# The attention-weighted sum of a windowed attention: one product of 64 keys per query block instead of two of 32

## What is computed

```python
# reference, cut: one layer of the macaron stage (DEPTH = 6 of them, run twice)
def attn_layer(x, Wqkv, qs, ksc, Wo):
    q, k, v = split(shift_tokens(x) @ Wqkv)         # 16 heads x 64
    q, k = rotary(l2norm(q) * qs), rotary(l2norm(k) * ksc)
    # windows of 32 tokens: a query block sees its own block and the one before it
    bk2, bv2 = look(blocks(k)), look(blocks(v))     # 64 keys for each block of 32 queries
    attn = softmax(where(mask, -max, einsum('bhwie,bhwje->bhwij', blocks(q), bk2) * 8.0))
    out = einsum('bhwij,bhwje->bhwie', attn, bv2)   # the product that is changed
    return merge(out) @ Wo
x = attn_layer(shift_tokens(x), ...) + x
x = ffn_layer(shift_tokens(x), ...) + x             # (a * gelu(gate)) @ W2
```

## Time and profile before

| | us |
|---|---|
| median of 3 executions | 4348.66 |
| lowest, highest | 4320.82, 4349.43 |
| the profiled execution, its own time | 4339.44 |
| span of the profiled execution | 4337.7 |
| first scores of the first and of the second macaron stage, from the span's start | 64.0, 1857.1 |
| granted TensorE clock, mean over the span | 0.959 |

### The profile page before, as it was taken

How to read it: one execution, slowest core, us unless ns; L and a number is a source line. 1 busy time by engine, 2 the same in 40 slices (tenths; PEclk the granted TensorE clock), 3 DMA queues, 4 the chain that set the end, 5 groups by cost and what they waited for, 6 DMA issues and landing times.

```text
span 4337.7 us, 161987 instructions
## 1 busy us (share of the span) xinstructions
PE 4006.5 (92%) x70897; PEld 2563.2 (59%) x70897; DVE 3070.5 (71%) x5228; ACT 2752.8 (63%) x4932; POOL 2741.4 (63%) x3746
## 2 busy tenths in 40 slices
PE   5999999999999999589999999999999976999985
PEld 3666666666666666356666666666666654333333
DVE  6777777777777776577777777777777744577744
ACT  3767677777767676167777767676777742366652
POOL 5877787777777776388777777777777750000000
PEclk8999999999999999799999999999999987599997
DMA  3000000000000000000000000000000000000000
GB/s 85 5 5 25 10 25 5 10 25 9 5 25 10 25 5 10 21 4 10 25 5 9 25 10 5 25 10 25 5 10 5 5 3 0 0 1 1 1 1 10
DMA packets 75304, 53.56 MB, mean 12 GB/s; under 512 B 48472, under 2 KB 71400, under 8 KB 72944
## 3 DMA queue, kind: packets, MB, share of 16 engines
q1 hardware_dynamic: 74608, 43.28, 3.6%
HBM read 35.93 MB, written 1.05 MB: 9 GB/s over the span
## 4 chain that ended last, share of the span: by engine, by line
PE 75%; DVE 13%; ACT 4%; issue 4%; POOL 3%; DVEq 0%; SPq 0%; POOLq 0%; DMA 0%; ACTq 0%
PE psum L339 12%; PE psum L404 8%; PE psum L350 8%; PE psum L361 8%; PE psum L423 7%; PE psum L386 5%; DVE turn L635 4%; PE psum L415 4%; PE psum L1155 3%; PE psum L503 3%; PE psum L493 3%; PE psum L486 3%; PE psum L1124 2%; DVE den L672 2%; PE psum L1143 2%
## 5 line engine op out<-in xcount | busy, mean ns | idle before, releaser
L635 DVE TENSOR_TENSOR turn<-psum,ropes 128x512 f32<-128x512 f32 x1536 | 946.5, 674 | 82.0 <-POOL qkr L736 53.3
L743 POOL TENSOR_TENSOR turn<-turn 128x1024 f32<-128x1024 f32 x384 | 903.7, 2376 | 8.3 <-DVE turn L635 8.2
L522 ACT ACTIVATE sq<-psum 128x512 f32<-128x512 f32 x768 | 455.5, 593 | 543.9 <-PE psum L339 543.9
L339 PE MATMUL psum<-wqkv,xT 128*128 128x512 f32 x1536 | 769.3, 624 | 8.6 <-DVE turn L635 6.6
L736 POOL TENSOR_TENSOR qkr<-turn,rn 128x1024 f32<-128x1024 f32 x384 | 727.2, 1914 | 1.0
L770 POOL TENSOR_TENSOR scratch<-scratch,rden 128x1024 f32<-128x1024 f32 x192 | 365.3, 1903 | 467.3 <-DVE rden L675 467.3
L404 PEld LDWEIGHTS psum<-scratch,V 32*64 32x64 f32 x29952 | 546.6, 132 | 182.4 <-issue 181.3
L404 PE MATMUL psum<-scratch,V 32*64 32x64 f32 (+1 forms) x29952 | 591.9, 222 | 6.3 <-issue 4.4
L361 PEld LDWEIGHTS psum<-ident,qkr 128*128 128x128 f32 x3072 | 325.9, 141 | 336.2 <-ACT kT L531 155.8
L361 PE MATMUL psum<-ident,qkr 128*128 128x128 f32 x3072 | 462.8, 283 | 11.7 <-POOL qkr L736 11.5
L350 PE MATMUL psum<-wqkv,xT 128*64 128x512 f32 x1536 | 415.4, 619 | 52.4 <-DVE turn L635 52.2
(11 more groups left out here) (182 smaller groups left out, 6518.0 us busy)
## 6 DMA issues: line engine op xcount, KB each, us to landing
wqkv<-in_L_ffn_Wqkv_dram SPq DMA_DIRECT2D x12, 1536.0 KB, 6.9
wo<-in_L_ffn_Wo_dram SPq DMA_DIRECT2D x12, 512.0 KB, 7.4
zs<-Y SPq DMA_DIRECT2D x192, 31.8 KB
w<-in_L_ffn_W_dram SPq DMA_DIRECT2D x12, 341.0 KB
zs<-Y SPq DMA_DIRECT2D x168, 0.2 KB
w<-in_L_ffn_W_dram SPq DMA_DIRECT2D x12, 128.0 KB
rope<-in_shape_consts_dram SPq DMA_DIRECT2D x1, 1024.0 KB
X<-in_L_attn_x_dram SPq DMA_DIRECT2D x2, 512.0 KB
```

The source lines that it names most:

```text
L339: pe.matmul(bank[b][:, :], xT[:, n // TPB % 2, bass.ts(n % TPB, P)], wqkv[n // TILES % 2][:, INNER * w:INNER * w + INNER].rearrange("p (h ...
L522: act.activation(sq[:, q // 2, q % 2, :, :], bank[QK_BANK[q]][:, :].rearrange("p (h d) -> p h d", d=RH), ACT.Square).then_inc(sem("squared ...
L635: e = dve.tensor_tensor(dst, src, tab.unsqueeze(1).broadcast_to([P, HEADS, RH]), ALU.mult)
L743: pool.tensor_tensor(t1, t1, turn2[:, w, :, :, :].rearrange("p a h d -> p (a h d)"), ALU.add).then_inc(sem("added"), 1)
```

## The change

`attend` now makes one product for each query block, head and head-pair side: 64 keys on 64 partitions (K = 64) against the 32 queries of one block, with start and stop in the same product. That is 64 products per tile for every tile, 32 in each call. The array is used as four quadrants of 64 x 64: rows 64e, output columns 64(e XOR x). The first call takes head indices i = 0, 1, the second i = 2, 3, so the wait on `half_attended` is gone; one `turn_qk` still stands between them.

For the odd query blocks (w = 1, 3) the two key blocks already lie side by side in V. For the even ones (w = 0, 2) they don't: a second buffer Vs holds them, with the block in front in the place of the odd window. SP fills it for each tile with six DMAs from V to Vs, 32 partitions each (two of 128 KB, four of 64 KB, 512 KB together), when the tile's values are there and the tile before is attended. PE waits for them ahead of `attend`.

Since the halves of the output now lie in other partitions for half of the heads, Wo's rows are loaded in another order, by four DMAs instead of one. To make room in the memory, three bias vectors of the last attention are loaded late into the place of w1, and onehotT moves into w1 as well. Three fewer DMAs stand in the initial load.

```diff
+        Vs = sb("Vs", [P, 2, PAIRS, DH])
...
-        LOADS = 16 * 22
+        LOADS = 16 * 19
...
-        bias = sb("bias", [P, 4, D])
+        bias = sb("bias", [P, D])
+        at_bias = w1[0][:, 0:3 * D].rearrange("p (a f) -> p a f", f=D)
...
-            for i, name in enumerate(("L0_attn_b_out", "L1_attn_b_o", "L1_attn_ln_g", "L1_attn_ln_b")):
-                sp.dma_start(bias[:, i, :], W[name].partition_broadcast(P)).then_inc(ld, 16)
+            sp.dma_start(bias[:, :], W["L0_attn_b_out"].partition_broadcast(P)).then_inc(ld, 16)
...
                 at = Counts(c)
+                pair_values(sp, at, 0)
                 for n in range(NT):
+                    if on(n + 1):
+                        pair_values(sp, at, n + 1)
                     shift_tile(sp, at, n)
...
+            sp.wait_ge(sem("unit_out"), Counts(1).group(NG - 5, "unit_out"))
+            for i, name in enumerate(("L1_attn_b_o", "L1_attn_ln_g", "L1_attn_ln_b")):
+                sp.dma_start(at_bias[:, i, :], W[name].partition_broadcast(P)).then_inc(sem("late_loaded"), 16)
...
+        def pair_values(sp, at, n):
+
+            to, done = Vs, sem("values_paired")
+            sp.wait_ge(sem("v_kept"), at.part(n, "v_kept", 1))
+            if n or at.macaron:
+                sp.wait_ge(sem("attended"), at.part(n - 1, "attended"))
+            for e in range(2):
+                even, odd = DH * e, DH * e + WIN
+                sp.dma_start(to[even:even + WIN, :, :, :], V[n % 3][even:even + WIN, :, :, :]).then_inc(done, 16)
+                sp.dma_start(to[odd:odd + WIN, 1, :, :], V[n % 3][odd:odd + WIN, 0, :, :]).then_inc(done, 16)
+                back = V[(n if starts_batch(n) else n - 1) % 3]
+                sp.dma_start(to[odd:odd + WIN, 0, :, :], back[odd:odd + WIN, 1, :, :]).then_inc(done, 16)
...
-            sp.dma_start(wo[i][:, :, :], W["Wo"][of, :, :].rearrange("(c p) f -> p c f", p=P)).then_inc(s, 16)
+            rows = W["Wo"][of, :, :].rearrange("(x i e d) f -> x e d i f", x=2, i=4, e=2)
+            for e in range(2):
+                for x in range(2):
+                    r0 = DH * (e ^ x)
+                    sp.dma_start(wo[i][r0:r0 + DH, 4 * e:4 * e + 4, :], rows[x, e, :, :, :]).then_inc(s, 16)
...
-                for i in range(4):
-                    for blk in range(-1, 4):
+                for i in (2 * half, 2 * half + 1):
+                    for w in range(BLK):
                         for x in range(2):
-                            s = half ^ x
-                            if blk % 2 != s or (blk < 0 and starts_batch(n)):
-                                continue
-                            p = 4 * x + i
-                            q0, q1 = max(WIN * blk, 0), min(WIN * blk + NWIN, P)
                             for e in range(2):
-                                r0 = DH * e + WIN * s
-                                v = V[(n if blk >= 0 else n - 1) % 3]
-                                mm = pe.matmul(bank[OUT_BANK[x]][DH * e:DH * e + DH, P * i + q0:P * i + q1],
-                                               v[r0:r0 + WIN, blk // 2 % 2, p, :], pT[r0:r0 + WIN, p, q0:q1],
-                                               start=first, stop=half == 1, skip_group_check=True)
-                mm.then_inc(sem("attended" if half else "half_attended"), 1)
+                                p, r0, o0 = 4 * x + i, DH * e, DH * (e ^ x)
+                                v = V[n % 3] if w % 2 else Vs
+                                rows = WIN if w == 0 and starts_batch(n) else NWIN
+                                mm = pe.matmul(bank[OUT_BANK[e]][o0:o0 + DH, P * i + WIN * w:P * i + WIN * w + WIN],
+                                               v[r0:r0 + rows, w // 2, p, :],
+                                               pT[r0:r0 + rows, p, WIN * w:WIN * w + WIN],
+                                               start=True, stop=True, skip_group_check=True)
+                if half:
+                    mm.then_inc(sem("attended"), 1)
...
                     pe.wait_ge(sem("v_kept"), part(o, "v_kept", 1))
+                    pe.wait_ge(sem("values_paired"), at.paired(o))
...
-                    pe.wait_ge(sem("half_attended"), part(o, "half_attended"))
                     attend(o, 1)
...
+            dve.wait_ge(sem("late_loaded"), 48)
```

More of the change, by code:

```diff
@@ L85, in step, with paired @@
         return self.macaron * STEPS + s - FIRST_STEP + 1
+    def paired(self, n):
+        return 96 * (self.macaron * NT + n + 1)
     def shifted(self, n):
@@ L190, in build @@
         onehot = sb("onehot", [P, 4, NE])
-        onehotT = sb("onehotT", [NE, 4, P], BF16)
+        onehotT = w1[1][0:NE, 0:2 * P].bitcast(BF16).rearrange("p (a t) -> p a t", t=P)
         stackc = sb("stackc", [P, 4])
@@ L272, in shift_tile @@
             sp.dma_start(z[0:1, :], row).then_inc(sem("shifted%d" % (n % 2)), 16)
+        def pair_values(sp, at, n):
[9 more added lines that the diff above has]
+                sp.dma_start(to[odd:odd + WIN, 0, :, :], back[odd:odd + WIN, 1, :, :]).then_inc(done, 16)
         zero_row = const[1:2, 384 + 4 * TPB * DH:384 + 4 * TPB * DH + HALF]
-        AW = 4
+        AW = 7
         def load_attention_weights(sp, layer):
@@ L389, in attend @@
             def attend(n, half):
-                for i in range(4):
-                    for blk in range(-1, 4):
+                for i in (2 * half, 2 * half + 1):
+                    for w in range(BLK):
                         for x in range(2):
-                            s = half ^ x
-                            if blk % 2 != s or (blk < 0 and starts_batch(n)):
-                                continue
-                            p = 4 * x + i
-                            q0, q1 = max(WIN * blk, 0), min(WIN * blk + NWIN, P)
-                            for e in range(2):
-                                r0 = DH * e + WIN * s
-                                v = V[(n if blk >= 0 else n - 1) % 3]
-                                first = half == 0 and i == 0 and blk == min(
-                                    k for k in range(-1, 4) if k % 2 == s and not (k < 0 and starts_batch(n)))
-                                mm = pe.matmul(bank[OUT_BANK[x]][DH * e:DH * e + DH, P * i + q0:P * i + q1],
-                                               v[r0:r0 + WIN, blk // 2 % 2, p, :], pT[r0:r0 + WIN, p, q0:q1],
-                                               start=first, stop=half == 1, skip_group_check=True)
-                mm.then_inc(sem("attended" if half else "half_attended"), 1)
+                            for e in range(2):
+                                p, r0, o0 = 4 * x + i, DH * e, DH * (e ^ x)
[7 more added lines that the diff above has]
+                    mm.then_inc(sem("attended"), 1)
             def turn_p(n, i):
@@ L913, in linear_dve @@
                 xs = X[:, bass.ds((TPB + 1) * b + 1, TPB), :]
-                dve.tensor_tensor(xs, xs, bias[:, 0, :].unsqueeze(1).broadcast_to([P, TPB, D]), ALU.add)
+                dve.tensor_tensor(xs, xs, bias[:, :].unsqueeze(1).broadcast_to([P, TPB, D]), ALU.add)
         ex_y = stage8[:, 0:4, :]
@@ L1300, in attention2_dve @@
             dve.wait_ge(sem("at_res"), 4)
-            dve.tensor_tensor(res, res, bias[:, 1, :].unsqueeze(1).broadcast_to([P, TILES, D]),
+            dve.wait_ge(sem("late_loaded"), 48)
+            dve.tensor_tensor(res, res, at_bias[:, 0, :].unsqueeze(1).broadcast_to([P, TILES, D]),
                               ALU.add).then_inc(sem("at_biased"), 1)
@@ L1316, in attention2_dve @@
             dve.wait_ge(sem("at_renormed"), TILES)
-            dve.tensor_tensor(res, res, bias[:, 2, :].unsqueeze(1).broadcast_to([P, TILES, D]),
+            dve.tensor_tensor(res, res, at_bias[:, 1, :].unsqueeze(1).broadcast_to([P, TILES, D]),
                               ALU.mult).then_inc(sem("at_scaled"), 1)
             dve.wait_ge(sem("at_scaled"), 1)
-            dve.tensor_tensor(res, res, bias[:, 3, :].unsqueeze(1).broadcast_to([P, TILES, D]),
+            dve.tensor_tensor(res, res, at_bias[:, 2, :].unsqueeze(1).broadcast_to([P, TILES, D]),
                               ALU.add).then_inc(sem("at_shifted"), 1)
```

## The result

| us | before | after |
|---|---|---|
| median of the runs taken side by side (17 and 17) | 4333.46 | 4320.25 |
| ratio, with its 95% interval | | 0.9959 [0.9943, 0.9975] |
| span of the profiled execution | 4337.7 | 4318.5 |
| up to the first scores of the first macaron stage | 64.0 | 58.1 |
| first macaron stage, its first to its 96th scores | 1647.1 | 1640.3 |

What follows compares the result with a forecast made beforehand. PE looked busiest, but its waits for DVE and a POOL-DVE loop were taken to limit the saving. Terms 24.5 + 8.0 + 1.3 = 33.8 us, from a 4348.7 median to about 4315; range 4285 to 4360.

Steps and rivals of the forecast that it cites:

- The product's price: Half of attend falls from 1.52 to 1.08 us if quadrants load independently; bounds 0.80 (scores' pace) and 2.01 (loads in turn).
- Where PE's saving ends: How much of the 0.88 us saved per tile arrives before PE's wait at L350 for DVE's rotate(u, 1), by step kind.
- O: Macaron-stage step of 18.05 us; DVE's second rotate limits its gain to 0.72 us, none before a new layer.
- N: Macaron-stage step of 15.38 us, forecast to gain 0.72 us and take 14.66.
- G: Step following the 15.38 us step; forecast to lengthen from 17.95 to 18.48 us, so the pair gains only 0.19.
- the loop of 15.9: POOL's adds, rsqrt and scale, then DVE's rotate and sums: 15.93 us from one normalising to the next.
- U: Macaron-stage step of 18.22 us, where PE already waits for DVE's rotate; forecast gain 0.
- Tightest is the O step ... I take 0: Copies to Vs queued behind weights: on time at full rate, late at quarter rate, 25 us at most; counted as 0.
- The two figures of that step: Tile wanted at 21.52 us after the scores; there by about 20.4 at full rate, 1.2 us late at a quarter.
- The counts: Steps multiplied by their gains: 34 x 0.72 = 24.5 us, and 42 pairs x 0.19 = 8.0 us.
- DMA traffic that slows others a little: One cause, slowing DVE or ACT, within the rival that nothing can be seen: 4340 to 4349 us, chance 0.19.
- the rival: The change does nothing that can be seen, 4340 to 4349 us, chance 0.19; the range takes it in.

## Why the prediction was half right

- *The product's price*: right. It went by the loads of one row group, 16 x 0.058 + 0.14 = 1.08, and 1.07 was measured. Both bounds, 0.80 and 2.01, were out. The Trainium skill's rule in TensorE: Matmul & The Clock Gate, Part 3 (The mechanism), that a load overlaps only products of another row group, is not borne out for quadrants with the same rows and other columns.
- *Where PE's saving ends*: right in each kind of step, to 0.05 us. O is set by DVE's second rotate, N is shortened, G takes back what the loop of 15.9 holds, U does not move. The runs with half the products and with two Newton steps show the first and the third by taking the suspected bound away.
- *"Tightest is the O step ... I take 0"*: this is the term that was mis-sized. It allowed 25 us for late values and took none of it. Behind the unit's weights the copies landed in time or at most some tenths late; behind the attention weights its own slow case came true: 7.7 to 8.9 us from the first issue to the last landing, with a room of 7.7, and 5.9 us in nine steps. What "hidden" left out is that the weights hold SP's queue ahead of the copies for 4.9 us (3.8 to 4.9 with Wo in one DMA), and then share the transfer engines with them. The copies as a whole cost 13 us in the profile with them taken out and 14 with them alone. The size of the copy itself was judged well: usual steps show no wait for it.
- *The two figures of that step* don't follow from the terms shown. Issue and transfer one after the other give 14.28 + 3.9 + 2.0 = 20.2 at the full rate, but 26.3, 4.8 us late, at a quarter of it; "1.2 us late" needs them to overlap. The measured 7.7 to 8.9 us lie near the overlapped 8.1.
- *The counts*: 34 O steps and 42 pairs take in steps at the ends of the stages that gain nothing; some 29 us instead of 32.5.
- *DMA traffic that slows others a little* stood in a rival as a small thing: it is 2.4 to 2.7 us in the scores. No engine's wait explains it.
- *The clock* was not in the sum. The prediction read 1.00 in every window of before and kept it, although the change turns busy time of PE into waits by design. Five falls cost 8 us here; half the products make it 198 us at the lower level in the two stages. This cuts against the bookkeeping "gain 0" for a step in which PE waits anyway: more waiting is not free there, though only long waits were seen to cost.
- *The initial load*: 1.3 for 5.9. The term was counted in issues (3 x 0.43) alone. The first scores come at 57.5 to 61.5 us in the ten profiles with the shorter load and at 61.0 to 64.0 in the three without, so 5.9 is one pair out of a scatter of 3 to 4 us; what beyond the issues went away was not followed up.
- *The steps before a new layer* were given gain 0, and rightly so, but their cause was read as DVE's 2.76 us alone. The exclusion between DVE and POOL stood in the trace of before, in POOL's offset of 2.91 us beside `scale_ropes`, and was not read.
- *The chances*: faster by over 1% was given 0.20, and nothing of what it needed occurred. The range of 75 us was set by the late values and the rival; it held. That the time came out near its middle is the luck told above.

## What to carry over

Before a saving on the busiest engine is multiplied by the number of steps, look for the wait that the saving will run into, in each kind of step, and price the neighbour's bound as well: here the same edit brought 18 us alone and 91 once two small neighbours (four POOL instructions, and the place of eight DVE ones) were out of the way. A DMA is hidden only if its turn in the issuing queue is: count what stands ahead of it there, and what it shares the transfer engines with. And where a saving becomes a wait of TensorE, leave something in the range for the granted clock.

## What the hardware showed unexpectedly

- Less work made the kernel slower. With half of the products out, PE waited more, the granted clock was down for 198 us in the two stages, and the time went up by 83. Part of it, in the steps before a new layer, is `scale_ropes` beside `scale`.
- Elementwise instructions of DVE with both inputs in the memory on the chip, and POOL's, hold each other up: eight of DVE take 2.76 us by themselves, 4.76 to 5.05 beside `scale`, and 0.27 us of POOL become 2.92. Beside POOL's small instructions of `rsqrt` the eight take only 3.06.
- Products on 32 and on 64 rows mixed: where a tile starts a batch, 8 of 32 products in a half have 32 rows, and the half takes 1.46 us, not 1.07. With 64 rows for all it is 1.07:

```profile
1213.39:1214.46 1.07, 1.07 (x64) 1.01 (x64) 1.00 0.00 0
```

The Trainium skill, TensorEngine Tiling (Array Packing), Key Properties, says that a change of tiling mode drains TensorE; less work taking 0.39 us longer agrees with that. In the U steps, where these tiles fall, PE waits anyway and it cost nothing.
- Weights of 2 MB in flight came together with PE standing still inside a block of 64 products, for 1.45 us, on no semaphore.
